# Retention layer and transformer layer on one core: matmuls on zeros at the start, row sums on two row groups, sums over sequences on consecutive words, and a new order

## The reference

```python
x = x + retention(layernorm(x), wq, wk, wv, wg, wo)
x = x + transformer(layernorm(x), ...)
...
# retention: 8 heads, key 16 and value 32 wide, along the 256 tokens
qk = einsum('bhik,bhjk->bhij', qr, kr) * mask          # decaying causal mask
qk = qk / clip(abs(qk.sum(-1)), 1.0)                   # row sums
out = rms(einsum('bhij,bhjd->bihd', qk, vr)); out = (silu(g) * out) @ wo
...
# transformer: attention runs over the 8 sequences (16 heads of 8, 4 for k and v, causal),
# each of the 256 tokens for itself
h1 = h + proj(softmax(q k^T) v)
# then 8 experts (128 -> 256 -> 128), top 2 of 8, capacity by rank among all tokens
return h1 + moe(layernorm(h1))
```

## Time and profile before

| what | us |
|---|---|
| median of 3 runs | 242.56 |
| lowest and highest | 239.9, 242.67 |
| the profiled execution | 242.57 |
| its span, first to last instruction | 240.8 |
| busy in it: TensorE | 216.7 |
| VectorE | 180.1 |
| ScalarE | 146.1 |
| GpSimd | 94.8 |

### The profile page before, as it was taken

The page is one execution under the profiler, slowest core; times in us unless marked ns, Lnnn a source line. Parts: engine busy times, 40 slices in busy tenths (PEclk is TensorE's granted clock), DMA queues, the critical chain, the costliest instruction groups (busy, mean ns, idle before and its releaser), DMA issues.

```text
span 240.8 us, 4945 instructions
## 1 busy us (share of the span) xinstructions
PE 216.7 (90%) x1744; PEld 183.6 (76%) x1744; DVE 180.1 (75%) x543; ACT 146.1 (61%) x268; POOL 94.8 (39%) x121
## 2 busy tenths in 40 slices
PE   0677868899999999989999999999999989989995
PEld 0456545688887878877888889998798869879994
DVE  1466788695989789899996998697749864895533
ACT  2162763778868756946973876586746465827431
POOL 0021345334558642528623850582465136521000
PEclk9977999999999999999999999999999999999999
DMA  6992000000000000000000000000000000000000
GB/s 178 292 319 57 4 0 0 4 0 3 0 3 3 0 25 0 3 1 3 1 0 25 0 0 4 22 3 0 22 3 1 23 0 4 22 3 0 23 3 22
DMA packets 8073, 6.46 MB, mean 27 GB/s; under 512 B 752, under 2 KB 7152, under 8 KB 8048
## 3 DMA queue, kind: packets, MB, share of 16 engines
q1 hardware_dynamic: 8048, 6.14, 8.8%
HBM read 5.09 MB, written 1.05 MB: 25 GB/s over the span
## 4 chain that ended last, share of the span: by engine, by line
PE 54%; DVE 16%; issue 14%; POOL 9%; ACT 4%; DMA 1%; DVEq 0%; POOLq 0%; ACTq 0%
PE bank L773 16%; PE bank L784 13%; POOL prod L293 5%; PE bank L672 3%; DVE ao L930 3%; PE bank L621 3%; PE bank L699 3%; PE bank L638 2%; DVE res L1036 2%; PE bank L684 2%; ACT L445 2%; POOL qk L369 2%; PE bank L629 1%; PE bank L691 1%; DVE sm L866 1%
## 5 line engine op out<-in xcount | busy, mean ns | idle before, releaser
L773 PE MATMUL bank<-x2T,w 128*128 128x256 f32 x256 | 64.4, 386 | 1.6 <-DVE res L1036 1.6
L784 PE MATMUL bank<-w,hT 128*128 128x128 f32 x512 | 64.7, 277 | 0.0
L784 PEld LDWEIGHTS bank<-w,hT 128*128 128x128 f32 x512 | 61.7, 192 | 3.0 <-issue 1.1
L583 ACT ACTIVATE hT<-bank 128x512 f32<-128x512 f32 x64 | 37.5, 598 | 23.6 <-PE bank L773 23.5
L773 PEld LDWEIGHTS bank<-x2T,w 128*128 128x128 f32 x256 | 45.3, 190 | 8.1 <-DVE res L1036 3.1
L1036 DVE SCALAR_TENSOR_TENSOR res<-bank,gate,res 128x128 f32<-128x128 f32 x128 | 38.4, 341 | 16.7 <-PE bank L784 15.4
L445 ACT ACT_TABLE_LOAD x36 | 46.2, 1283 | 4.4 <-DVE mv L812 3.7
L293 POOL TENSOR_TENSOR prod<-qkv 128x128 f32<-128x128 f32 (+7 forms) x16 | 22.3, 1413 | 36.6 <-ACT qkv L455 36.6
L866 DVE TENSOR_TENSOR sm<-bank,con 128x512 f32<-128x512 f32 x32 | 19.9, 683 | 5.1 <-PE bank L672 5.0
L301 POOL TENSOR_TENSOR prodv<-attn_exp,qkv 128x128 f32<-128x128 f32 (+7 forms) x16 | 18.7, 1188 | 9.2 <-ACT attn_exp L551 9.2
L376 POOL TENSOR_TENSOR qkc<-qk,kcum 128x256 f32<-128x256 f32 x8 | 5.8, 730 | 31.0 <-DVE kcum L852 31.0
(11 more groups left out here) (109 smaller groups left out, 378.8 us busy)
## 6 DMA issues: line engine op xcount, KB each, us to landing
x<-in_x SPq DMA_DIRECT2D x8, 128.0 KB, 4.3
w<-in_w SPq DMA_DIRECT2D x1, 1024.0 KB, 5.8
out<-res SPq DMA_DIRECT2D x8, 128.0 KB, 1.8
con<-in_consts SPq DMA_DIRECT2D x1, 512.0 KB, 4.2
con<-in_consts SPq DMA_DIRECT2D x1, 256.5 KB, 4.3
con<-in_consts SPq DMA_DIRECT2D x1, 256.0 KB, 4.4
rcon<-in_rconsts SPq DMA_DIRECT2D x1, 132.0 KB, 2.9
wqk<-in_wqk SPq DMA_DIRECT2D x1, 128.0 KB, 2.2
```

The lines of the kernel that those rows point to most:

```text
L583: eng.activation(hT[:, n % NM], m_banks[n % NM][:].rearrange("p (t n) -> p t n", t=NF), ACT.Gelu_apprx_tanh).then_inc(sem("gelu"), 1)
L773: last = mm(m_banks[n % NM][:, t * SLEN:(t + 1) * SLEN], w1[:, e, t * P:(t + 1) * P], x2T[:, i], start=True, stop=True)
L784: last = mm(m_banks[n % NM][:, c * D:(c + 1) * D], hT[:, n % NM, t, c * P:(c + 1) * P], w2[:, e, t], start=(t == 0), stop=(t == NF - 1))
```

## The change

It does six things.

1. A tile `warm` of zeros is set by VectorE, and a new stage `p_warm` multiplies it with itself into an expert bank, eight times: four ahead of the first transpose, four among the first stages. Nobody reads the result.
2. In `a_rstd` ScalarE loads its table before it waits for the statistics.
3. For sequences 0 and 1 VectorE does `a_qkc`, `a_weight`, `b_core`, `b_prod` and `b_prodv`, and `b_core` there reads x1 and the mean directly and doesn't wait for `b_sub`.
4. `a_rowsums` makes its two halves from 64 rows each, the lower and the upper half of the array, into two banks (`f0` and `f1`, now one tensor `front`), instead of from all 128 rows into one bank. So it waits for `silu`, which `a_scores` waited for.
5. `sc`, `scm`, `attn_exp` and `prodv` lie with the row of the sequence innermost: `b_max`, `b_sum` and `b_ao` reduce consecutive words; `b_scores` writes at a stride, and `value_product` reads the values at a stride of 192 words.
6. `ORDER` is a new table.

```diff
...
+p_warm:0 p_warm:1 p_warm:2 a_stats:0 p_warm:3 a_aggr:0 a_rstd:0 a_xh:0 a_T:0 a_xT:0 a_qk:0 a_vmm:0 a_rotate:0
+p_warm:4 a_v:0 a_g:0 a_rotated:0 a_stats:1 a_tanh:0 a_kT:0 p_warm:5 a_kcum:0 a_qo:0 a_knat:0 a_silu:0
...
@@ -203,6 +204,7 @@
         before = sb("before", [P, 2 * P], BF16)
         expert_no = rcon[:, 2 * P:]
         eps = sb("eps", [P, 2])
+        warm = sb("warm", [P, SLEN])
 
         x = sb("x", [P, NSEQ, NC, D])
         x1 = sb("x1", [P, NSEQ, NC, D])
@@ -275,7 +277,9 @@
         hT = sb("hT", [P, NM, NF, SLEN])
         res = sb("res", [P, NSEQ, NC, D])
 
-        ps = [ctx.enter_context(nc.psum_tensor(f"bank{i}", [P, 512], F32)) for i in range(8)]
+        front = ctx.enter_context(nc.psum_tensor("bankf", [P, 2, 512], F32))
+        ps = [front[:, 0], front[:, 1]] + [ctx.enter_context(nc.psum_tensor(f"bank{i}", [P, 512], F32))
+                                           for i in range(2, 8)]
         f0, f1, k0, k1 = score_banks = ps[:4]
         b_banks = [ps[4 + i % NB] for i in range(NSEQ)]
         m_banks = ps[4 + NB:4 + NB + NM]
@@ -299,9 +303,11 @@
 
             n = i + 1
             return eng.tensor_tensor(
-                prodv[:, c, 0:n * D].rearrange("p (a d) -> p a d", d=HD),
-                attn_exp[:, c * n * NH:(c + 1) * n * NH].unsqueeze(2).to_broadcast([P, n * NH, HD]),
-                qkv[:, c, 0:n, D + KVD:QKV].unsqueeze(2).to_broadcast([P, n, QPK, KVD]), ALU.mult)
+                prodv[:, c, 0:n * D].rearrange("p (h d t) -> p h d t", d=HD, t=n),
+                attn_exp[:, c * n * NH:(c + 1) * n * NH].rearrange("p (h t) -> p h t", t=n)
+                .unsqueeze(2).to_broadcast([P, NH, HD, n]),
+                qkv[:, c, 0:n, D + KVD:QKV].rearrange("p t f -> p f t")
+                .unsqueeze(1).to_broadcast([P, QPK, KVD, n]), ALU.mult)
 
 
         @block.sync
@@ -370,12 +376,16 @@
                                   ALU.add).then_inc(sem("rotated"), 1)
 
             def a_qkc(i):
+                if i < VECTOR_FIRST:
+                    return
                 eng.wait_ge(sem("kcum"), i + 1)
                 if i >= 1:
                     eng.wait_ge(sem("rowsum"), i)
                 eng.tensor_tensor(qkc[:], qk[:, i % 2, 0], kcum[:], ALU.mult).then_inc(sem("qkc"), 1)
 
             def a_weight(i):
+                if i < VECTOR_FIRST:
+                    return
                 eng.wait_ge(sem("rs"), i + 1)
                 eng.wait_ge(sem("silu"), i + 1)
                 eng.tensor_tensor(wgt[:], rs[:], silu[:, i % 2], ALU.mult).then_inc(sem("wgt"), 1)
@@ -457,10 +473,10 @@
             def a_rstd(i):
 
                 group = next(g for g in RSTD_GROUPS if g[0] == i)
+                exp_ln()
                 eng.wait_ge(sem("a_aggr"), NC * (group[-1] + 1))
                 if i == 0:
                     eng.wait_ge(sem("eps"), 2)
-                exp_ln()
                 js = slice(group[0], group[-1] + 1)
                 eng.activation(lnv[:, js], mv[:, js, :, 1], ACT.Ln, bias=eps[:, 0:1]).then_inc(sem("a_lnv"), 1)
                 eng.wait_ge(sem("a_lnv"), RSTD_GROUPS.index(group) + 1)
@@ -503,7 +519,7 @@
                 eng.wait_ge(sem("rowsum"), i + 1)
                 if i >= 2:
                     eng.wait_ge(sem("tt"), i - 1)
-                eng.activation(s2[:, i % 2], f1[:], ACT.Square, scale=EPS ** 0.5).then_inc(sem("s2"), 1)
+                eng.activation(s2[:, i % 2].rearrange("p (u n) -> p u n", u=2), front[:, :, 0:SLEN], ACT.Square, scale=EPS ** 0.5).then_inc(sem("s2"), 1)
 
             def a_osq(i):
                 eng.wait_ge(sem("o"), i + 1)
@@ -598,6 +614,12 @@
         def _(eng):
             mm = eng.matmul
 
+            def p_warm(i):
+
+                if i == 0:
+                    eng.wait_ge(sem("warm"), 1)
+                mm(m_banks[0][:, 0:SLEN], warm[:, 0:P], warm[:], start=True, stop=True)
+
             def a_T(i):
                 if i < VECTOR_FIRST:
                     eng.wait_ge(sem("xh_v"), NC * (i + 1))
@@ -651,14 +673,15 @@
             def a_rowsums(i):
                 eng.wait_ge(sem("qkc"), i + 1)
                 eng.wait_ge(sem("state"), i + 1)
+                eng.wait_ge(sem("silu"), i + 1)
                 for u in range(2):
-                    last = mm(f1[:, u * SLEN:(u + 1) * SLEN], same_head[:, u * P:(u + 1) * P], qkc[:],
+                    rows = slice(u * D // 2, (u + 1) * D // 2)
+                    last = mm(front[:, u, 0:SLEN], same_head[rows, u * P:(u + 1) * P], qkc[rows, :],
                               start=True, stop=True)
                 last.then_inc(sem("rowsum"), 1)
 
             def a_scores(i):
                 eng.wait_ge(sem("qo"), i + 1)
-                eng.wait_ge(sem("silu"), i + 1)
                 eng.wait_ge(sem("s2"), i + 1)
                 if i >= 1:
                     eng.wait_ge(sem("x1"), i)
...
@@ -800,6 +823,7 @@
         @block.vector
         def _(eng):
             tt_, ts_ = eng.tensor_tensor, eng.tensor_scalar
+            eng.memset(warm[:], 0.0).then_inc(sem("warm"), 1)
 
             def a_stats(i):
                 eng.wait_ge(sem(f"x{i}_in"), 16)
@@ -851,6 +875,44 @@
                     eng.wait_ge(sem("qkc"), i)
                 eng.tensor_tensor_scan(kcum[:], carry, qk[:, i % 2, 1], 0.0, ALU.mult,
                                        ALU.add).then_inc(sem("kcum"), 1)
+
+            def a_qkc(i):
+                if i < VECTOR_FIRST:
+                    eng.wait_ge(sem("kcum"), i + 1)
+                    if i >= 1:
+                        eng.wait_ge(sem("rowsum"), i)
+                    tt_(qkc[:], qk[:, i % 2, 0], kcum[:], ALU.mult).then_inc(sem("qkc"), 1)
+
+            def a_weight(i):
+                if i < VECTOR_FIRST:
+                    eng.wait_ge(sem("rs"), i + 1)
+                    eng.wait_ge(sem("silu"), i + 1)
+                    tt_(wgt[:], rs[:], silu[:, i % 2], ALU.mult).then_inc(sem("wgt"), 1)
+
+            def b_core(i):
+                if i < VECTOR_FIRST:
+                    eng.wait_ge(sem("b_rstd"), i + 1)
+                    if i >= 1:
+                        eng.wait_ge(sem("b_T"), i)
+                    for c in range(NC):
+                        last = ts_(core[:, c], x1[:, i, c], bmv[:, i, c, 0:1], br[:, i, c, 1:2], ALU.subtract, ALU.mult)
+                    last.then_inc(sem("core"), 1)
+
+            def b_prod(i):
+                if i < VECTOR_FIRST:
+                    eng.wait_ge(sem("qkv_in_sb"), i + 1)
+                    if i >= 1:
+                        eng.wait_ge(sem("sc"), NC * i)
+                    for c in range(NC):
+                        key_product(eng, i, c).then_inc(sem("prod"), 1)
+
+            def b_prodv(i):
+                if i < VECTOR_FIRST:
+                    eng.wait_ge(sem("b_exp"), i + 1)
+                    if i >= 1:
+                        eng.wait_ge(sem("ao"), NC * i)
+                    for c in range(NC):
+                        value_product(eng, i, c).then_inc(sem("prodv"), 1)
 
             def a_state(i):
                 eng.wait_ge(sem("state_ps"), i + 1)
@@ -896,28 +958,29 @@
                     eng.wait_ge(sem("scm"), i)
                 for c in range(NC):
                     eng.wait_ge(sem("prod"), NC * i + c + 1)
-                    eng.tensor_reduce(sc[:, c * n * NH:(c + 1) * n * NH],
-                                      prod[:, c, 0:n * D].rearrange("p (a d) -> p a d", d=HD),
+                    eng.tensor_reduce(sc[:, c * n * NH:(c + 1) * n * NH].rearrange("p (h t) -> p t h", t=n),
+                                      prod[:, c, 0:n * D].rearrange("p (t h d) -> p t h d", t=n, d=HD),
                                       X, ALU.add).then_inc(sem("sc"), 1)
 
             def b_max(i):
                 n = i + 1
                 eng.wait_ge(sem("sc"), NC * n)
-                s = sc[:, 0:NC * n * NH].rearrange("p (c t h) -> p c t h", c=NC, t=n)
-                eng.tensor_reduce(mx[:], s.rearrange("p c t h -> p c h t"), X, ALU.max).then_inc(sem("mx"), 1)
+                s = sc[:, 0:NC * n * NH].rearrange("p (a t) -> p a t", t=n)
+                eng.tensor_reduce(mx[:].rearrange("p c h -> p (c h)"), s, X, ALU.max).then_inc(sem("mx"), 1)
                 eng.wait_ge(sem("mx"), n)
                 if i >= 1:
                     eng.wait_ge(sem("b_exp"), i)
-                tt_(scm[:, 0:NC * n * NH].rearrange("p (c t h) -> p c t h", c=NC, t=n), s,
-                    mx[:].unsqueeze(2).to_broadcast([P, NC, n, NH]), ALU.subtract).then_inc(sem("scm"), 1)
+                tt_(scm[:, 0:NC * n * NH].rearrange("p (a t) -> p a t", t=n), s,
+                    mx[:].rearrange("p c h -> p (c h)").unsqueeze(2).to_broadcast([P, NC * NH, n]),
+                    ALU.subtract).then_inc(sem("scm"), 1)
 
             def b_sum(i):
                 n = i + 1
                 eng.wait_ge(sem("b_exp"), n)
                 if i >= 1:
                     eng.wait_ge(sem("aon"), i)
```

(6 more changed lines are left out.)

144 lines of the change are left out of this document (72 added, 72 removed).

## The result

The changed kernel takes 248.94 us (median of 4 runs, 246.13 to 250.01) against 241.23 us for the kernel before (239.81 to 242.67): ratio 1.027, 95% interval 1.018 to 1.035. Forecast were 237.5 us and a range up to 243. Timed again on another chip it took 244.22 us (244.16 to 246.26) against 242.35, ratio 1.014, interval 1.005 to 1.023. Runs of either kernel differ by stretches at the lower clock level that come and go, and a ratio leaves out the runs that such a stretch disturbed most, so it isn't the quotient of the medians. Side by side on the second chip, where the granted clock reads 1.00, the spans are 242.4 to 244.5 us for the changed kernel and 237.9 to 239.2 for the one before, 4.4 to 5.3 us apart. It is slower, by 1 to 3%: both intervals lie above 1, and neither lies wholly above 1.02.

A forecast was written before the change was run, and what follows sets the result against it. It took a latency-bound head, then from 53.5 us a TensorE lacking only 5.5 us. 240.8 - 0.3 - 2.3 - 1.2 + 0.3 - 1.6 = 235.7 us span, plus 1.8 gives 237.5 us; range 231.5 to 243.

The forecast's parts named there:

- the layout: Sums on consecutive words: `ao` saves 2.8 us on the chain, the strided value product costs 3.0; net +0.3 us.
- work ahead: New order up to `b_T:1`: TensorE does output products and groups of later sequences before it, saving 2.3 us.
- row sums: 64-row halves side by side on TensorE: 0.24 us saved a pair, 1.2 us for sequences 3 to 7.
- freed waits: TensorE's wait for accumulations (`res`) before an `m_fc1` goes as VectorE is freed of first `ao` chunks: 1.6 us off.
- Value product: factor 1.2: GpSimd's strided value product takes 1.2 times as long, by the key product's row, 2362 against 1974 ns; costs 3.0 us.
- The rival at factor 1.5: Strided value product costs half as much again, `res` waits stay: +4.5 and +1.6 us, 243.6 us, no change; chance 0.10.
- the sum by that rule alone: Row sums if a tiling mode change drains the array: a pair gains 0.05 us, the forecast 1.0 us higher.
- The wait for `silu`: Now ahead of the row sums pair; costed at nothing, at most 0.68 us where the gate's VectorE step is late.
- Head: Up to `b_T:1`: first transpose near 5.0, `b_T:0` 5.3 us earlier at 29.5, `b_T:1` at 53.2, 0.3 us saved.
- `scm`: One-row VectorE step of 697 ns; new products of its form might be held 0 to 0.5 us each, left in range.
- Slower: The outcome of a measurement above 247.4 us, beyond about 2% from no change; chance 0.06.
- The two rivals that named the mechanism: Strided value product at factor 1.5 (243.6 us, chance 0.10) or above (245.1 at 1.6, 251 at 2.0; chance 0.07).

The follow-up runs named there:

- x_oldsums: Changed kernel with its sums over sequences in the old layout again, the value product reading contiguous values; 244.77 us.
- x_values_t: Changed kernel with the values copied once by ScalarE, row innermost, so the value product reads consecutive runs; 243.05 us, ratio 1.011 to before.
- b_zeros: Kernel before, in its own order, with only the early table load and the eight products on zeros; 239.62 us, ratio 0.9953.
- x_again: The changed kernel unaltered, timed again on another chip; 244.22 us against 242.35 for before, ratio 1.014.
- b_newsums: Kernel before with only the new layout of sums on consecutive words and the strided value product; 245.82 us, ratio 1.020.
- x_steps_gpsimd: Changed kernel with the five VectorE steps of sequences 0 and 1 back on GpSimd, in the new order; 255.63 us, ratio 1.057.

## Why the prediction was wrong

It forecast 182.5 us from `b_T:1` to the end; it took 191.1, the 185.4 of the table and 5.7 of tail. The 8.6 us are of two kinds. TensorE's work fell by 1.1 instead of 2.3 + 1.2 = 3.5 us: 2.4. Its idle time rose by 4.9 instead of falling by 1.3 (the 1.6 for `res` less the 0.3 of the layout): 6.2.

By its terms: the layout, forecast at +0.3 us, costs 2.5 (x_oldsums), which is 2.2 of the 8.6. The other 6.4 are there with the old layout too: 182.9 us behind `b_T:1`, where work ahead (2.3), row sums (1.2) and freed waits (1.6) should have left 176.5. The premise under all of these failed: that from `b_T:1` on time follows the sum of TensorE's work, with the attention hidden behind it. In the new order the six loops from `b_T:2` on follow the attention chain, to 0.02 us where its products change. Of the whole 8.6 us, 5.0 go with the stride; the cause of the other 3.6 is open.

- *Value product: factor 1.2.* The first step that failed, mis-sized. The 1.2 was right for what its row could show, a product without inner broadcast (2359 ns); the stride came on top, to 1.45 at eight rows and 1.53 at seven. For four to eight rows the products took 7.1 us more than before, where the prediction had 3.0. The prediction held both prices and took the nearer row, when the operation had lost the broadcast and gained a stride. The rival at factor 1.5 priced it at +4.5 and +1.6 us; x_values_t gives 5.0 for the stride, with 2.3 of `res` in it. The Trainium skill's GPSIMD Engine Reference (Performance pitfalls for Q7 kernels) has half as much again for a read over 8 bytes. The traces show less for the stride alone, 1.21 to 1.30 against the copied values; 1.45 to 1.53 (five to eight rows) is the stride with the lost broadcast.
- *Idle before `m_fc1`: 1.6 us off.* Failed with it: VectorE waits for the second chunk in `ao`, with `res` behind; 4.2 us. Freeing VectorE is worth nothing where it then waits. The order has a part in it too: with the old sums 2.5 us stay, with copied values 1.9.
- *Row sums: 0.24 us a pair.* 0.05 behind `b_T:1`, where the prediction had 1.2 us in all. The Trainium skill's TensorEngine Tiling (Key Properties) has the array drain on a change of mode, and the sum by that rule alone gave exactly 0.05. The trace agrees in that the way in costs about what the way out costs, 0.09 and 0.11 us, though the pair itself took 0.63 us and not 0.43. The wait for `silu`, put at nothing, came to 0.6 us, once.
- *Work ahead of `b_T:1`: 2.3 us.* The instructions are ahead (1392 left instead of 1427), but with the row sums' share they bring only 1.1 us, and hardly any time: with the stride gone the new order needs 180.4 us, 1.2 less than before and 0.5 less than b_zeros, and idles 5.9. One place is visible: between `c_T:6` and `b_T:7` the new order has three `m_fc2` and two `m_fc1`, 5.73 us, the old one two `m_fc1` and 3.78 us. Whether that alone is the loss is open; moving three of them didn't show it.
- *Head.* Right in x_again: first transpose 5.01, first query/key product 1.13 us, `b_T:0` 29.46 for 29.5. Between `b_T:0` and `b_T:1` it was 21.8 us for 23.7: VectorE was busy 20.0 of them, 0.5 under the walk, and waited 1.8 instead of 3.2. In the first profile the clock rose later, and both errors cancelled: 53.23 for 53.2 is luck. What the zeros are worth against before was overrated: the profile of before held lower clock that many of its runs don't have (its span 240.8, clock 0.986; others 238.0, clock 1.00).
- *`scm`*: 191 ns instead of 697. It is the place in the order and not the layout: 193 ns in x_oldsums (old layout, new order), 695 in b_newsums (new layout, old order).
- *Chances.* Slower had 0.06. The two rivals that named the mechanism had 0.17 together, for a price that they themselves put at 1.5 and 1.6. The forecast started from 242.56 us, a median with lower clock in it; where its clock reads 1.00, before mostly has 239.7 to 240.0.

## What to carry to other kernels

Price a changed access pattern by all that changes in it, each factor by its own row, and multiply; a layout that makes a reduction cheap can make its producer pay, and when the producer is the slower engine on the chain, the consumer only waits. A TensorE that is busy for most of a stretch doesn't have to be what sets its length: vary a link of the other chain and see whether the stretch moves with it. Work moved ahead is not time saved: ask what each serial chain behind it waits for. Compare kernels by stretches of the trace at the same granted clock before explaining a few us between medians.

## What the hardware showed that was not expected

- GpSimd's product of two inputs: 1974 ns for 1024 words with an inner broadcast, 2359 without, 2866 with one input at a stride of 192 words. The broadcast is worth 1.2 there and nothing at four rows (1072 and 1079 ns; 1.14 to 1.25 at three and at five to seven); the stride costs 1.21 to 1.30 times at every size from three rows to eight (974 to 1240 ns at three).
- With the same eight products on zeros, the clock rose in time for the first transpose in one execution and 5 us later in another. `b_T:1` without them came 3.6 us later than the one and 5.6 later than the other.
- In x_steps_gpsimd TensorE idled 5.47 us up to 31.9 us, and the clock column reads 0.51 and 0.50 in the two stretches of 5 us from 30 us on. That wait cost more than its length.
- The clock column can miss the lower level: it reads 1.00 in the head of the changed kernel, where a group takes 2.07 us in one execution and 1.13 in the other.
- Small VectorE operations with two inputs are held in some places and not in others, at the same size: the value product of one row (128 words) took 278 ns in the changed kernel and 918 ns in x_values_t, which only reads its values elsewhere; `gsel` (16 words) 177 ns in b_zeros and 1290 ns once in before. What held them was not tried, and in x_values_t the lost time grew from 1.3 us on VectorE to 2.6 us in its loop.
